# Bias adds on VectorE, one more tile ahead, and adapter products between the halves of a tile: two feed-forward stages of a macaron block

## The reference

```python
x = x + 0.5 * ffn(layernorm(x))
x = x + attention(layernorm(x))
x = x + 0.5 * ffn(layernorm(x))

def ffn(x):                      # x: (2, 1024, 1024)
    y = einsum('bsd,od->bso', x, weight) + bias
    # one of 3 adapters of rank 16 (or none) for each of the 2 batch rows
    lo = einsum('bsr,bor->bso', einsum('bsd,brd->bsr', x, A), Bw)
    return y + where(use_lora, lo, 0)
```

## Time and profile before

| what | value |
|---|---|
| median of 3 runs | 1855.8 us |
| profiled execution | 1856.24 us, its span 1854.4 us |
| TensorE busy | 1764.4 us (95%) |
| VectorE busy | 1275.2 us (69%) |
| ScalarE busy | 1009.4 us (54%) |
| GpSimd busy | 816.1 us (44%) |
| first stage | 0 to about 233 us |
| second stage | about 1649 to 1854 us |
| bias adds on GpSimd from the third tile on | 28 of 2.55 us mean |

### The profile page before, as it was taken

One profiled execution on the slowest core, in us unless ns is written; L12 is line 12 of the kernel. 1 busy time (PEld: TensorE's weight loads), 2 busy tenths in 40 slices (PEclk: granted clock), 3 DMA queues, 4 the chain that ended last, 5 costly groups with the idle time before them and its releaser, 6 DMA issues. The chain is left out here.

```text
span 1854.4 us, 43454 instructions
## 1 busy us (share of the span) xinstructions
PE 1764.4 (95%) x15248; PEld 1396.4 (75%) x15248; DVE 1275.2 (69%) x2482; ACT 1009.4 (54%) x2137; POOL 816.1 (44%) x585
## 2 busy tenths in 40 slices
PE   5899969899999999999999999998999999988898
PEld 4688869777777777777777777775788888866787
DVE  5687458778788787888878888788533444337774
ACT  2221057788888888888889888886200011112210
POOL 3232212467676766767667676773200000022322
PEclk9999989999999999999999999999999999999999
DMA  6876463412222122221222212227755655526654
GB/s 218 285 243 184 136 183 97 82 59 88 58 65 82 58 77 64 68 82 58 63 69 78 82 58 57 66 81 234 284 196 202 205 209 184 193 104 225 201 177 144
DMA packets 161312, 245.65 MB, mean 132 GB/s; under 512 B 30432, under 2 KB 114528, under 8 KB 159200
## 3 DMA queue, kind: packets, MB, share of 16 engines
q1 hardware_dynamic: 161248, 244.80, 41.8%
HBM read 153.78 MB, written 76.28 MB: 124 GB/s over the span
## 5 line engine op out<-in xcount | busy, mean ns | idle before, releaser
L1384 PE MATMUL psS<-keyT,q 128*128 128x512 f32 (+2 forms) x2304 | 462.1, 348 | 12.6 <-issue 3.4
L1384 PEld LDWEIGHTS psS<-keyT,q 128*128 128x128 f32 x2304 | 377.2, 190 | 95.4 <-issue 33.2
L1502 DVE CUSTOM_DVE_ANT_0 prob<-psS,mask 128x640 f32<-128x640 f32 (+7 forms) x512 | 380.3, 750 | 79.6 <-PE psS L1384 54.9
L1512 DVE STREAM_TRANSPOSE pT<-prob 128x640 f32<-128x640 f32 (+7 forms) x512 | 375.1, 761 | 82.0 <-PE psV L1401 77.5
L1451 ACT ACTIVATE prob<-prob,negmax 128x640 f32<-128x640 f32 (+7 forms) x512 | 393.3, 769 | 66.8 <-DVE negmax L1502 62.4
L1177 PE MATMUL psS<-o_w,o_o 128*128 128x512 f32 x1536 | 353.0, 392 | 4.9 <-DVE o_w L1145 4.2
L1177 PEld LDWEIGHTS psS<-o_w,o_o 128*128 128x128 f32 x1536 | 290.5, 189 | 67.1 <-issue 5.6
L515 PE MATMUL f_psy<-f_weff,f_xT 128*128 128x512 f32 x1344 | 316.8, 397 | 12.2 <-DVE f_xT L613 9.1
L515 PEld LDWEIGHTS f_psy<-f_weff,f_xT 128*128 128x128 f32 x1344 | 254.9, 190 | 73.4 <-DVE f_xT L613 12.5
L1401 PE MATMUL psV<-pT,val 32*64 32x512 f32 (+3 forms) x8192 | 264.5, 407 | 7.2 <-DVE pT L1512 4.7
L699 POOL TENSOR_TENSOR pT<-pT,cosT 64x512 f32<-64x512 f32 x124 | 160.1, 1291 | 244.9 <-ACT pT L694 235.6
(11 more groups left out here) (124 smaller groups left out, 1735.2 us busy)
## 6 DMA issues: line engine op xcount, KB each, us to landing
o_parts<-pT SPq DMA_DIRECT2D x128, 256.0 KB, 3.0
wo<-in_wo SPq DMA_DIRECT2D x16, 1024.0 KB, 5.0
o_in<-o_parts SPq DMA_DIRECT2D x32, 512.0 KB, 6.5
o_o<-o_parts SPq DMA_DIRECT2D x32, 512.0 KB, 7.5
o_o<-row_scales SPq DMA_DIRECT2D x32, 512.0 KB, 8.3
f_xt<-in_x SPq DMA_DIRECT2D x16, 512.0 KB, 4.3
f_w_in<-in_w SPq DMA_DIRECT2D x16, 512.0 KB, 6.8
w_sum<-f_w_in SPq DMA_DIRECT2D x16, 512.0 KB, 5.8
```

Of the source, the lines that this page charges most:

```text
L1384: ins = nc.tensor.matmul(psS[:, slot, start + x0:start + x1], q[:, e, a, t * P:(t + 1) * P], k.keyT[:, m, b * S + x0:b * S + x1], start=(i ...
L1502: nc.vector.tensor_tensor_reduce(out=prob[:, n % RING, 0:width], in0=place(n), in1=k.mask[:, S - width:S], scale=-1.0, scalar=LARGEST, op0 ...
L1512: nc.vector.transpose(pT[:, n % 2, t, 0:width], prob[:, n % RING, 0:width]).then_inc(turned, 1)
```

## The change

Four things change, all in `ffn_phase` and `ffn_steps`.

1. The bias of tiles 2 to 15 is added by VectorE. In step n it adds the bias of tile n+1, behind the first half's result of tile n. It waits there for `xo_in`, the load of tile n+1 into `f_xo`, which SyncE issues in the same step n.
2. Pieces 9 to 15 are spread otherwise: piece 8 is summed in the head ahead of `flip(2)`, step 2 has piece 9, step 3 piece 10, step 4 pieces 11 and 12, steps 5 to 7 pieces 13 to 15. TensorE forms the product of a step's piece between the two halves of its tile, that of piece 12 behind tile 4. VectorE sums a piece behind the first half's result, and makes its low part (odd pieces) behind the bias add (in the first stage behind the flip as well).
3. In the second stage everything up to the moves is a tile further ahead: step n transposes n+2, normalises n+3, takes the statistics of n+4. SyncE loads x of n+4 first and then moves n+3.
4. TensorE starts a tile when its high part is there and waits for the low part only ahead of the second of the three products.

```diff
-    step(1, 1, 0, range(DT, AHEAD), has(1))
+    step(1, 1, 0, (DT,), has(1))
     for n in range(2, NT // 2):
-        step(n, n % 2, 0, range(n + DT, n + DT + 1), has(n))
+        first = n + DT - 1 if n <= 4 else n + DT
+        step(n, n % 2, 0, range(first, first + (2 if n == 4 else 1)), has(n))
...
             def step(n, j, b, pieces, has):
                 if not later(n, 2):
                     sp.wait_ge(result, 2)
                     sp.dma_start(dst_d[0:P, :], xo[:, 0, :]).then_inc(stored[0], 16)
-                if has(2):
-                    move(n + 2, j)
-                if has(4):
+                if has(4) and ahead == 2:
+                    load_x(n + 4, j)
+                if has(1 + ahead):
+                    move(n + 1 + ahead, (j + 1 + ahead) % 2)
+                if has(4) and ahead == 1:
                     load_x(n + 4, j)
...
         def _(pool):
             def add_bias(n, j):
-                if later(n, 2):
-                    pool.wait_ge(xo_in[j], (n - j) * 8)
-                    nc.gpsimd.tensor_tensor(xo[:, j, :], xo[:, j, :], bias_half[:], ALU.add).then_inc(with_bias, 1)
-                    return
...
             def step(n, j, b, pieces, has):
                 pieces_low(pieces)
-                if has(1):
-                    add_bias(n + 1, (j + 1) % 2)
...
+                pe.wait_ge(f.hi, n * 2 + 2)
+                pe.wait_ge(result, n * 2 - 2)
+                if b == 1:
+
+                    pe.wait_ge(w_lo[0], PIECES // 2)
+                    pe.wait_ge(w_lo[1], PIECES // 2)
+                for half in range(2):
+                    for i, (a, m) in enumerate(PASSES):
+                        if half == 0 and i == 1:
+                            pe.wait_ge(f.lo, n * 2 + 2)
...
+                    ins.then_inc(product, 1)
+                    for i in pieces[half:half + 1]:
                         outer_products(i)
...
+            make_pieces([DT])
             flip(2, 0)
+            if ahead == 2:
+                f.stats_of(nc, dve, 4, 0, loads_of(4, 0))
...
-                if has(2):
-                    normalised(n + 2, j)
-                make_pieces(pieces)
-                if has(3):
-                    f.stats_of(nc, dve, n + 3, jm, loads_of(n + 3, jm))
+                if has(2) and ahead == 2:
+                    flip(n + 2, j)
+                if has(1 + ahead):
+                    normalised(n + 1 + ahead, ja)
+                if has(2 + ahead):
+                    f.stats_of(nc, dve, n + 2 + ahead, (ja + 1) % 2, loads_of(n + 2 + ahead, (ja + 1) % 2))
                 results(n, j, [0])
-                if has(2):
+                sum_pieces(pieces[:1])
+                if not later(n, 2):
+                    results(n, j, [1])
+                if has(1):
+                    dve.wait_ge(xo_in[jm], loads_of(n - 1, jm if later(n, 2) else 0))
+                    nc.vector.tensor_tensor(xo[:, jm, :], xo[:, jm, :], bias_half[:], ALU.add).then_inc(with_bias, 1)
+                if has(2) and ahead == 1:
                     flip(n + 2, j)
-                results(n, j, [1])
+                low_pieces(pieces[:1])
+                if later(n, 2):
+                    results(n, j, [1])
+                make_pieces(pieces[1:])
```

More of the change, by code:

```diff
@@ L313, in move @@
                 if later(m, 3):
+                    sp.sem_inc(f.passed, 1)
                     sp.wait_ge(flipped, m - 2)
@@ L361, in _ @@
                     load_x(4, 0)
+            if ahead == 2:
+                move(3, 1)
             def step(n, j, b, pieces, has):
@@ L449, in _ @@
                     f.root_of(nc, act, k.eps_ln[:], i - 2, i % 2)
+            if ahead == 2:
+                f.root_of(nc, act, k.eps_ln[:], 4, 0)
             def step(n, j, b, pieces, has):
@@ L458, in step @@
                 pieces_hi(pieces)
-                if has(3):
-                    f.root_of(nc, act, k.eps_ln[:], n + 3, (j + 1) % 2)
+                if has(2 + ahead):
+                    f.root_of(nc, act, k.eps_ln[:], n + 2 + ahead, (j + ahead) % 2)
             ffn_steps(act, step)
@@ L501, in step @@
             def step(n, j, b, pieces, has):
-                for i in pieces:
-                    if i > DT:
-                        outer_products(i)
[L505 to L517, removed]
-                        ins.then_inc(product, 1)
+                if not later(n, 2):
+                    return
+                pe.wait_ge(f.hi, n * 2 + 2)
[7 more added lines that the diff above has]
+                            pe.wait_ge(f.lo, n * 2 + 2)
+                        for dt in range(DT):
+                            ins = nc.tensor.matmul(psy[:, j, half, :], f.xT[:, j, a, dt, :],
+                                                   weff[:, b, m, dt, half * BANK:(half + 1) * BANK],
+                                                   start=(i == 0 and dt == 0), stop=(i == 2 and dt == DT - 1))
+                    ins.then_inc(product, 1)
+                    for i in pieces[half:half + 1]:
+                        outer_products(i)
             ffn_steps(pe, step)
@@ L529, in make_pieces, with low_pieces @@
                                                 w_in[:, i % SLOTS, :], ALU.add).then_inc(summed, 1)
+            def low_pieces(pieces):
+                for i in pieces:
                     if i % 2 == 1:
@@ L532, in make_pieces @@
                         low(nc.vector, i)
+            def make_pieces(pieces):
+                for i in pieces:
+                    sum_pieces([i])
+                    low_pieces([i])
             def choose():
@@ L603, in _ @@
                     normalised(2, 0)
+                if i == 6 and ahead == 2:
+                    normalised(3, 1)
+            make_pieces([DT])
             flip(2, 0)
+            if ahead == 2:
+                f.stats_of(nc, dve, 4, 0, loads_of(4, 0))
             def step(n, j, b, pieces, has):
@@ L608, in step @@
                     results(0, 0)
-                jm = (j + 1) % 2
+                    pieces = ()
+                jm, ja = (j + 1) % 2, (j + 1 + ahead) % 2
                 if has(1):
@@ L614, in step @@
                                                 ALU.subtract).then_inc(f.lo, 1)
-                if has(2):
-                    normalised(n + 2, j)
-                make_pieces(pieces)
-                if has(3):
-                    f.stats_of(nc, dve, n + 3, jm, loads_of(n + 3, jm))
-                results(n, j, [0])
-                if has(2):
+                if has(2) and ahead == 2:
+                    flip(n + 2, j)
+                if has(1 + ahead):
+                    normalised(n + 1 + ahead, ja)
+                if has(2 + ahead):
+                    f.stats_of(nc, dve, n + 2 + ahead, (ja + 1) % 2, loads_of(n + 2 + ahead, (ja + 1) % 2))
+                results(n, j, [0])
+                sum_pieces(pieces[:1])
+                if not later(n, 2):
+                    results(n, j, [1])
[3 more added lines that the diff above has]
+                if has(2) and ahead == 1:
                     flip(n + 2, j)
-                results(n, j, [1])
+                low_pieces(pieces[:1])
+                if later(n, 2):
+                    results(n, j, [1])
+                make_pieces(pieces[1:])
             ffn_steps(dve, step)
```

2 lines of the change are left out of this document (1 added, 1 removed).

## The result

The changed kernel takes 1906.1 us (median of 4 runs, 1905.7 to 1907.9). The kernel before took 1856.7 us on the same chip. The ratio is 1.0266, 95% interval 1.0248 to 1.0284: slower by 49 us. The forecast was 1897, so its sign and its main mechanism are borne out and its size is 9 us short.

The account below looks back on a forecast made before the run. With the change, a chain through VectorE's wait for the load into f_xo was to bound both feed-forward stages. First stage +23.7 and second +17.3 make +41.0 on 1856.24: 1897 us, 8-in-10 range 1873 to 1909.

Parts of the forecast that it names:

- The step that carried it: Both feed-forward stages: VectorE waits in step n for a load issued behind that step's moves, making a chain; +41.0 us.
- The step of the first stage's loop: First stage, tiles 8 to 15: the chain of links takes 13.7 us a step against TensorE's 11.22 a tile.
- the signs that I had named: Adds idle 3 to 5 us, tiles 14 to 15 apart, gaps of 10 or more ahead of tile 8, tile 2 near 61.8.
- The landing: Both stages: time from issue of the load into f_xo to the waiting add's start; bounds 3.50 and 5.49 us.
- the first rival: Load into f_xo lands early, in 3.50 us in every step of both stages: +17.8, 1874 us; chance 0.18.
- step 4: First stage, the step with a second piece's sum: 16.6 us, against 14.3 for an even piece and 15.4 for odd.
- operations that shut each other out, costed at nothing: GpSimd's low part of an even piece could lock out VectorE's moved add; costed at nothing, 10 us if it met it.
- the third rival: Both stages: long stalls cost clock, 1.6 us once or twice, and lockout may join; +41 + 3 + 7, 1907 us; chance 0.12.
- low pairs at 1.27 throughout: Sign: VectorE's pair of low parts takes 1.27 us everywhere, not the 3.52 seen beside GpSimd's bias add.
- a chain that catches up with the last two tiles: First stage, tiles 8 to 15: the lead covers the 13.7 chain for some five tiles; the last two lose about 1.3 us.
- rows that overlap: Deduction for rows overlapping successors: about 0.2 us a step in the first stage, putting tile 8 at 165.2 instead of 166.4.
- The second (the wait is hidden): Load is there by VectorE's wait for the first half; loop 11.1 us, TensorE decides both stages; 1836 us; chance 0.05.

Follow-up runs that it names:

- where the load stands first: Changed kernel with the load of tile n+1 into f_xo ahead of the moves and the x load in SyncE's step; 1899.5 us, ratio 1.0217.

## Why the prediction came out as it did

**The step that carried it held.** VectorE's adds wait 120.4 us in 28 waits, on a load issued in the same step. The step of the first stage's loop was forecast at 13.7 and took 13.6, and the second stage's step 2 was forecast to begin 49.7 us behind the stage's first transpose (1699.0 less 1649.3) and began at 50.2 (1731.83 less 1681.63). The kernel before with part 1 alone (+2.6%) and the version with the add a step later (-0.2%) show it by taking the wait in and out. Of the signs that I had named, the adds' idle times are 5.4 us on average in the first stage and 3.2 in the second (3 to 5 forecast), and tile 2 starts at 63.00 (61.8 forecast).

**The landing.** I took 5.49 in the first stage with weight traffic, 4.45 in its loop and 4.65 in the second stage. In six of the seven unrolled steps it was 5.4 to 5.7 (first: 70.21 to 75.64), in the loop 4.4 to 4.6, and in most steps of the second stage 3.9 to 4.2, in two of them 5.0. One was longer, in step 3 of the first stage: issued at 100.00 and seen at 106.53, 6.53. Why that one is longer stays open. The page of the Trainium skill that the first rival names (DMA: Bandwidth & Descriptors, "Anatomy of one DMA — SWDGE (gpsimd) path") gives its sum for DMAs that GpSimd issues, and these are issued by SyncE; its 3.2 us is still near the 3.1 to 3.5 of the loads with little in front of them.

**First term that was mis-sized: step 4.** It took 18.05 where I had 16.6. The second piece makes ScalarE round piece 12 ahead of the tile's high part, and VectorE waits another 1.83 us for that. I had counted VectorE's own work for the second piece and not its place in ScalarE's order.

**Second: operations that shut each other out, costed at nothing.** I said that GpSimd's low part comes 4 us before the add. In the first stage it does so twice (100.78 and 151.07, 5.8 and 4.4 us ahead of an add), and twice it meets other operations than the add. VectorE and GpSimd of the changed kernel, first stage:

```profile
64.23 2.70 DVE L574 TENSOR_SCALAR f_xn<-f_xt,f_mv,f_rstd 128x1024 f32<-128x1024 f32 x1
...
127.72 2.90 DVE L631 TENSOR_TENSOR f_xT<-f_xn,f_xT 128x512 fp32r<-128x512 f32 x2 [1.83 <-ACT f_xT L459]
```

```profile
63.95 2.42 POOL L297 TENSOR_TENSOR f_weff<-f_w_in,f_weff 128x1024 fp32r<-128x1024 f32 x1 [9.27 <-ACT f_weff L432]
...
127.06 2.41 POOL L297 TENSOR_TENSOR f_weff<-f_w_in,f_weff 128x1024 fp32r<-128x1024 f32 x1 [23.86 <-ACT f_weff L432]
```

The normalise takes 2.70 where 0.81 is the median, the low pair 2.90 where it takes 1.28. Both are links of the chain: 1.9 + 1.6 = 3.5 us. In the second stage the pair at 1757.64 took 3.48 and the weight's low part at 1785.04 took 3.36, with GpSimd's low parts at 1757.62 and 1784.69: 2.2 + 2.1 = 4.3. That is 7.8 us in all, which I had bounded by 10 and put into the third rival; my sign "low pairs at 1.27 throughout" did not come. The rule of the Trainium skill (SBUF: State Buffer, "SBUF: two separate sides") agrees with these four places, as far as rows beside each other show it. No run here took GpSimd's low parts away, so that they are the cause in these places is read, not tested. What was tested is GpSimd's add of the same shape: with it gone from the kernel before (the version with a late bias add), none of the 56 low parts of a tile is long, where 13 were. And what I had feared for the moved add happens in two other versions: beside a low part of GpSimd's at 94.49 the add took 3.14 us at 94.86 where the load stands first, and three of the 28 adds took 3.22 in the kernel before with a late bias add.

**Third: the clock.** TensorE's granted clock in the changed kernel, in stretches of 11.3 us from tile 8 on (columns: PE busy and matmuls, PEld, DVE, ACT, POOL, granted clock, DMA share, GB/s):

```profile
173.40:184.70 11.30, 11.24 (x40) 8.97 (x41) 5.11 (x10) 0.34 (x2) 0.00 (x0) 0.80 0.65 187
184.70:196.00 11.30, 11.30 (x50) 9.08 (x49) 6.89 (x11) 1.45 (x3) 0.00 (x0) 1.00 0.51 138
```

Behind 14.91 us without a matmul the mean clock of the stretch is 0.80 of full, and it runs 40 matmuls where the next has 50 at 1.00: 10 / 50 x 11.3 = 2.3 us. In narrower stretches the clock is 1.00 at 159 to 160 us, 0.50 at 165 to 166 and still 0.50 from 173.46 to 177.46, then 1.00 from 178.46 on: TensorE fell to the lower of its two levels (1.2 GHz) within the wait and came back to the upper one (2.4 GHz) behind 11 matmuls, which started 0.43 us apart where later ones are 0.23 apart. That is the first stage's growth from tile 8 on (32.8 - 30.7 = 2.1). My forecast had 1.3 there for another reason, a chain that catches up with the last two tiles. It did not: TensorE runs on without a gap, and the last tile's low part was there in time, since the last two steps, in which no x load stands ahead of the load into `f_xo`, took 12.3 us (228.56 to 240.89 to 253.18) and not the loop's 13.7. The number was near, its reason wrong. In the second stage tile 8 takes 12.35 us from its first matmul to the next tile's behind 11.62 us of waiting, where each later tile takes 10.88: 1.5 us more. The slow matmuls ahead of tile 8 (7.25 instead of 5.84 at 79.32) cost nothing, since the chain decides there.

**The sum.** The first stage's tile 8 was 8.3 late against the forecast. The first add is seen at 75.64 where I took 72.45: 1.3 because VectorE's first low pair began later (62.78 for 61.48), 1.9 because of the long normalise. Step 3 adds 1.3, most of it the landing; step 4 adds 1.45; step 5 adds 1.2, the long pair. The last 1.2 is what I had taken off for rows that overlap: steps 2 and 6 took 15.29 and 14.25 where the links without that deduction give 15.4 and 14.3. The second stage's tile 8 was 3.1 late: 4.3 of long operations and 0.5 for the later step 2, less 1.5 for the landings (about 4.1 in four steps and 5.0 in two, where I had 4.65); 0.2 is left over. From tile 8 on the first stage lost 0.8 more than I had put there, and the second 1.1 less. That 1.1 is made of two terms that I had wrong: I took the first stage's 11.22 for a tile of the second, where the earlier trace rows give 43.77 / 4 = 10.94 and the changed kernel takes 10.88, 2.6 too much for eight tiles, and I left out the 1.5 of the clock. 41.0 + 8.3 + 3.1 + 0.8 - 1.1 = 52.1, against 51.6 measured.

**The rivals.** The first (the load lands in 3.50) did not come: only the last loads of a stage, with little in front, came in under 3.9. The second (the wait is hidden) is shown false by 28 idle times. The third, clock and lockout together, gave 1907, and the kernel took 1906: by size it was the better forecast, with a lockout of 7.8 us where it put 7 and a clock that cost 2.1 + 1.5 = 3.6 where it put 3. That it came within 1 us is partly luck. The rest of its sum was the forecast's, which was some 5.5 us too short in the head, the steps 3 and 4, the deduction and the second stage's start, and some 5.5 too long in the second stage's landings and tiles and in the chain that was to catch up.

**Where I was wrong about the rest of the change.** I took parts 2 to 4 for a gain that the load hides, and in the first two expectations for 15 to 20 us to be had without it. They cost 9 us by themselves. With a late bias add the kernel takes 1848 (ratio 0.9958) without them and 1855 (0.9984) with them, and 1846 (0.9944) once the second stage's low parts of pieces stand ahead of the statistics. The first and the last are not to be told apart, since the intervals of their ratios overlap. What was gained lay in taking the add off GpSimd without its wait.

## What to carry to other kernels

When an operation moves to another engine, its wait moves with it and holds up all that stands behind it there; read from the trace how long the old engine stood waiting, and place the operation as late in the new engine's order as its reader allows. Here GpSimd stood waiting for 113 us in the second stage alone, and VectorE waited only 0.7 us for its adds. As VectorE's own, the wait for the same loads cost 49 us of the kernel; the same add one step later made a gain of 0.4%. The same holds inside an order that is kept: a result that is due at one fixed point (piece 15's low part at tile 8) belongs ahead of every wait that has nothing to do with it.

## What the runs showed of the hardware that was not expected

- A load into `f_xo` of 512 KB was seen landed 3.1 us after its issue at the end of the first stage (255.85 to 258.99) and 3.4 to 3.5 at the end of the second, with nothing or little in front; 3.9 to 5.0 behind the moves of its step; and 5.4 to 6.5 with weight traffic as well. All these loads have one size, so what else is in the queues changes the time by up to a factor of two; which transfer does it was not tested.
- VectorE's normalise, with one tensor in SBUF and two values for each partition, was held up by GpSimd like operations with two tensors (2.70 for 0.81 us; in the kernel before 2.6 to 3.0 in 14 of 32). It is also quick for its width, 0.81 where the add of the same 128 x 1024 takes 1.22. The Trainium skill (SBUF: State Buffer, "SBUF: two separate sides") puts operations in a two-port mode beside those with two inputs in SBUF, which would fit the first number; that such a mode is what makes it quick, no run here shows.
- In the two feed-forward stages of the ten traces, 114 operations of VectorE took over 1.3 times the shortest of their kind (normalises, low parts of tiles and of pieces, bias adds), and each of them has an operation of GpSimd beside it. Operations that read one of their tensors from PSUM (the results and the sums of pieces), the transposes and the statistics were never long, though 143 of them ran beside GpSimd's for 0.15 us or more.
- Behind the two longest waits TensorE ran at the lower level of its clock at first and then at the upper: 11 matmuls of 0.43 us and 2.1 us lost behind 14.91 us of idle time, 7 such matmuls and 1.5 us lost behind 11.62.
